# One more step of lag for the head's sums, eight row places instead of four, and an expert number read earlier, in a fused tower of transformer, retention block and mixture of experts

## What is computed

```python
h = tok_ref(x, ...)                                  # 2 layers, band attention, D=192, then LN and a head to 128
h = h + attn_ref(_layernorm(h), ...)                 # retention block, below
h = h + ffn_ref(_layernorm(h), ...)                  # 8 experts, top 1, below

# attn_ref, on x of 128 columns
xn = layernorm(x, ln1_g, ln1_b)
s = a * s + (1 - a) * xn_t                           # scan over time, then ss @ W_out.T + b_out
y_loc = conv(xn, conv_w, 5 taps, per column)
x = x + ss @ W_out.T + b_out + y_loc + conv_b
h = gelu(layernorm(x, ln2_g, ln2_b) @ W1.T + b1)     # 256 wide
x = x + h @ W2.T + b2

# ffn_ref
scores = softmax(xf @ Wg + bg); top_s, top_i = top_k(scores, 1)
out = relu(xf @ W1[e] + b1[e]) @ W2[e] + b2[e]       # e = top_i of the token, 512 wide
return out * top_s
```

## Time and profile before

| what | value |
|---|---|
| time, median of 3 runs (lowest to highest) | 946.12 us (945.46 to 947.41) |
| the profiled execution: its own time / its span | 946.6 us / 944.8 us |
| busy share of the span: PE, PEld, DVE, ACT, POOL | 86%, 66%, 62%, 62%, 59% |
| final stream, from the first sums to the last scatter | 759.6 to 870.3 us |
| tile loop, from the first load's issue to the end | 873.2 to 944.8 us |
| DMA `xt<-xs`: count, issue to landing (min / median / max) | 23, 2.0 / 2.0 / 2.9 us |
| DMA `out<-ot`: count, issue to landing (median) | 23, 2.3 us |

### The profile page before, as it was taken

How to read it: one execution, slowest core, us unless ns; L and a number is a source line. 1 busy time by engine, 2 the same in 40 slices (tenths; PEclk the granted TensorE clock), 3 DMA queues, 4 the chain that set the end, 5 groups by cost and what they waited for, 6 DMA issues and landing times.

```text
span 944.8 us, 23661 instructions
## 1 busy us (share of the span) xinstructions
PE 815.0 (86%) x8467; PEld 619.5 (66%) x8467; DVE 589.8 (62%) x1891; ACT 585.4 (62%) x1622; POOL 553.4 (59%) x819
## 2 busy tenths in 40 slices
PE   5969998999999899898999899999988938983776
PEld 2757767567777565677775567777665727772675
DVE  3868846448987364488873626888534346897343
ACT  3859985248799842378997435799964124662453
POOL 4638876443588664556886625378855355676233
PEclk9989997999999999999999999999989958996899
DMA  2310000602000006120000141100004150001221
GB/s 66 102 43 4 3 16 8 190 6 74 4 3 3 21 23 190 28 85 8 4 3 21 51 141 49 32 4 3 3 3 132 58 202 1 1 29 62 66 74 38
DMA packets 38597, 43.85 MB, mean 46 GB/s; under 512 B 7163, under 2 KB 33882, under 8 KB 38346
## 3 DMA queue, kind: packets, MB, share of 16 engines
q1 hardware_dynamic: 18348, 19.40, 6.8%
q10 hardware_dynamic: 17860, 18.19, 6.1%
q0 software_dynamic: 2272, 4.74, 1.6%
HBM read 20.70 MB, written 21.59 MB: 45 GB/s over the span
## 4 chain that ended last, share of the span: by engine, by line
PE 59%; DVE 13%; ACT 9%; issue 5%; SPq 4%; DMA 4%; POOL 4%; ACTq 1%; POOLq 0%; DVEq 0%
PE bank L1338 7%; PE bank L1475 6%; PE bank L1499 5%; PE bank L1426 4%; PE bank L1544 4%; PE bank L1545 4%; PE bank L1478 3%; PE bank L1364 3%; ACT p L732 3%; PE bank L1375 3%; PE bank L1429 3%; DMA xt<-xs 2%; SPq L453 2%; DVE p L993 2%; PE bank L1390 1%
## 5 line engine op out<-in xcount | busy, mean ns | idle before, releaser
L568 POOL TENSOR_TENSOR p<-p 128x384 f16<-128x384 f32 (+1 forms) x320 | 270.8, 859 | 114.1 <-ACT p L732 105.6
L986 DVE TENSOR_REDUCE nmx<-bank 128x1 f32<-128x384 f32 (+1 forms) x384 | 191.2, 513 | 40.2 <-PE bank L1429 36.1
L731 ACT ACTIVATE p<-bank 128x384 f32<-128x384 f32 (+1 forms) x384 | 174.1, 453 | 46.2 <-PE bank L1478 32.5
L732 ACT ACTIVATE p<-bank 128x384 f16<-128x384 f32 (+1 forms) x384 | 174.1, 453 | 0.0
L1475 PE MATMUL bank<-stack 103*128 103x128 bf16 x1056 | 145.4, 222 | 7.4 <-DMA stack<-mtr 6.0
L1478 PE MATMUL bank<-bandb,idb 128*128 128x128 bf16 x672 | 135.5, 222 | 0.0
L1426 PE MATMUL bank<-stack 100*128 100x384 bf16 (+1 forms) x384 | 120.7, 314 | 1.6 <-DVE nmx L986 1.3
L1499 PE MATMUL bank<-vst,p 128*128 128x49 bf16 x2112 | 115.6, 185 | 1.7 <-POOL p L568 1.7
L1475 PEld LDWEIGHTS bank<-stack 103*128 103x128 bf16 x1056 | 88.4, 99 | 32.0 <-issue 15.6
L1429 PE MATMUL bank<-bandb,idb 128*128 128x128 bf16 x672 | 101.2, 220 | 0.0
L1499 PEld LDWEIGHTS bank<-vst,p 128*128 128x128 f16 x2112 | 91.8, 97 | 11.5 <-POOL p L568 2.1
(11 more groups left out here) (252 smaller groups left out, 1809.7 us busy)
## 6 DMA issues: line engine op xcount, KB each, us to landing
xs<-zrow ACTq DMA_DIRECT2D x8, 2193.0 KB, 11.9
xt<-xs SPq DMA_DIRECT2D x23, 129.0 KB, 2.0
w2s<-in_w SPq DMA_DIRECT2D x4, 576.0 KB
mwbs<-in_mwb SPq DMA_DIRECT2D x1, 2064.0 KB, 8.9
mw2s<-in_mw SPq DMA_DIRECT2D x1, 2048.0 KB, 13.2
lnrow<-in_lnr SPq DMA_DIRECT2D x4, 480.0 KB
stack<-mtr SPq DMA_DIRECT2D x96, 3.0 KB
w1b<-in_w SPq DMA_DIRECT2D x4, 291.0 KB
```

The costliest lines, as they stand in the source:

```text
L568: nc.gpsimd.tensor_tensor(p2[:, u % RING, 0:w], p32[:, u % RING, 0:w], p1[:, u % RING, 0:w], ALU.subtract).then_inc(p2_pool, 1)
L731: nc.scalar.activation(p32[:, s % RING, 0:w], ps[2 + s % 3][:, 0:w], ACT.Exp).then_inc(p32_ready, 1)
L732: nc.scalar.activation(p1[:, s % RING, 0:w], ps[2 + s % 3][:, 0:w], ACT.Exp).then_inc(p1_ready, 1)
L986: nc.vector.tensor_reduce(nmx[:, vn % 3, h:h + 1], nat_bank(v)[:, 0:w], AX.X, ALU.max, negate=True).then_inc(max_done, 1)
```

## The change

Three things, and nothing in the computed values:

1. `DEPTH` goes from 12 to 13, and each lag from that of the head's sums on grows by one on all engines (2 to 3, 3 to 4, and so on up to 12 to 13). The lags of `resid`'s sums (0) and of `z0`, its transposes, `xa`, `xb`, the head's product and `h0` (1) stay. The stream has 29 steps.
2. `XBUF` goes from 4 to 8.
3. In the tile loop VectorE reads the expert number of tile `i + 1` behind `dest` of tile `i`, ahead of its wait for the second product.

```diff
-XBUF, WBUF, OBUF = 4, 3, 4
+XBUF, WBUF, OBUF = 8, 3, 4
...
-DEPTH = 12
+DEPTH = 13
...
@@ VectorE, final stream
-                    i = t - 2
+                    i = t - 3
                     if 0 <= i < NN:
                         dve.wait_ge(kept, i + 1)
                         s_link = ch.mark(nc.vector.bn_stats(sums[:, 1, :], h0[:, i, :]))
...
-                i = t - 4
+                i = t - 5
                 if 0 <= i < NN:
                     b, n = divmod(i, NB)
                     dve.wait_ge(a1_done, i + 1)
...
@@ TensorE, final stream
-                i = t - 5
+                i = t - 6
                 if 0 <= i < NN:
                     b, n = divmod(i, NB)
                     pe.wait_ge(a1_done, min(i + 2, (b + 1) * NB))
...
-                    if t - 8 >= 0:
-                        pe.wait_ge(a2_done, t - 7)
+                    if t - 9 >= 0:
+                        pe.wait_ge(a2_done, t - 8)
...
@@ VectorE, tile loop
+            def expert(i):
+                return dve.value_load(toi[0:1, 0, i:i + 1], min_val=0, max_val=E - 1)
+
+            e = expert(0)
             for i in range(NT + 2):
                 if i < NT:
-                    e = dve.value_load(toi[0:1, 0, i:i + 1], min_val=0, max_val=E - 1)
                     if i >= WBUF:
                         dve.wait_ge(e_relu, i - WBUF + 1)
...
+                if i + 1 < NT:
+                    e = expert(i + 1)
                 if i >= 2:
```

More of the change, by code:

```diff
@@ L614, in _ @@
                     nc.gpsimd.tensor_tensor(x1[:, i, :], x1[:, i, :], bo2b[:, 0, :], ALU.add).then_inc(xb_ready, 1)
-                i = t - 7
+                i = t - 8
                 if 0 <= i < NN:
@@ L803, in _ @@
             for t in range(NN + DEPTH):
-                i = t - 8
+                i = t - 9
                 if 0 <= i < NN:
@@ L816, in _ @@
                                          scale=lfb[0:DHI, 0:1]).then_inc(a0_done, 1)
-                i = t - 3
+                i = t - 4
                 if 0 <= i < NN:
@@ L831, in _ @@
                                          scale=l12[:, 2:3]).then_inc(a2_done, 1)
-                i = t - 11
+                i = t - 12
                 if 0 <= i < NN:
@@ L1115, in _ @@
                 w, p = t % 2, (t - 1) % 2
-                i = t - 6
+                i = t - 7
                 if 0 <= i < NN:
@@ L1120, in _ @@
                     nc.vector.tensor_tensor(x1[:, i, :], ps[4][:, 0:DM], x1[:, i, :], ALU.add).then_inc(y_added, 1)
-                i = t - 10
+                i = t - 11
                 if 0 <= i < NN:
@@ L1581, in _ @@
                     pe.wait_ge(z0_ready, i + 1)
-                    if t - 8 >= 0:
-                        pe.wait_ge(a2_done, t - 7)
+                    if t - 9 >= 0:
+                        pe.wait_ge(a2_done, t - 8)
                     nc.tensor.transpose(ps[0][0:DLO, 0:P], z0[:, i % 2, 0:DLO], idf[:, :])
                     nc.tensor.transpose(ps[0][0:DHI, P:2 * P], z0[:, i % 2, DLO:D], idf[:, :]).then_inc(t0_mm, 1)
-                i = t - 3
+                i = t - 4
                 if 0 <= i < NN:
                     pe.wait_ge(z1_ready, i + 1)
-                    if t - 12 >= 0:
-                        pe.wait_ge(a3_done, t - 11)
+                    if t - 13 >= 0:
+                        pe.wait_ge(a3_done, t - 12)
                     nc.tensor.transpose(ps[1][:, 0:P], z1[:, i % 2, :], idf[:, :]).then_inc(t1_mm, 1)
-                i = t - 12
+                i = t - 13
                 if 0 <= i < NN:
@@ L1599, in _ @@
                         ins.then_inc(lg_mm, 1)
-                i = t - 9
+                i = t - 10
                 if 0 <= i < NN:
@@ L1620, in _ @@
                     nc.tensor.transpose(ps[0][:, 0:P], z2[:, i % 2, :], idf[:, :]).then_inc(t2_mm, 1)
-                i = t - 11
+                i = t - 12
                 if 0 <= i < NN:
                     pe.wait_ge(z3_ready, i + 1)
-                    pe.wait_ge(a1_done, min(t - 2, NN))
+                    pe.wait_ge(a1_done, min(t - 3, NN))
                     nc.tensor.transpose(ps[1][:, 0:P], trow[:, i, 0:DM], idf[:, :]).then_inc(t3_mm, 1)
```

## The result

| | before | after |
|---|---|---|
| time, median (lowest to highest) | 946.76 us, 4 runs (945.46 to 948.02) | 923.98 us, 4 runs (921.13 to 925.23) |
| the profiled execution: own time / span | 946.6 / 944.8 us | 924.96 / 923.2 us |
| ratio, 95% interval | | 0.9755 (0.9726 to 0.9784) |

A forecast was written before the change was run, and what follows sets the result against it. Bound by a ring of VectorE, TensorE and ScalarE in the stream's opening and by late row loads in the tile loop; 4.3 + 13.1 = 17.4 us off the median 946.12 gives 928.7 us, range 924.0 to 936.0.

The forecast's parts named there:

- the ring of two engines: Stream's opening: closed loop of VectorE's `z0`, TensorE's products and ScalarE's copies back to VectorE's sums, 4.43 us a step.
- Opening: Stream's steps 1 to 8: lagging the head's sums makes tapless steps 2.57 us, 23.65 instead of 27.67, gaining 4.02 us.
- the bound of 7.6: Stream up to the tile loop: upper bound of its gain, 7.6 us, if the clock rises before the taps.
- I let it keep that place: End of the stream's steps: `choose` still starts 0.50 us ahead of its step's head product, 4.0 us earlier than before.
- Eight places: Tile loop: loads run eight tiles ahead, tiles take 2.00 us instead of 2.72, tile 20 comes 12.4 us earlier.
- because it is the distance measured within a pair: Tile loop: reason for pricing a tile at 2.00 us, as TensorE starts tile 11 2.00 us behind tile 10.
- The lower bound of 1.96: Tile loop: TensorE's own work, 7.22 us busy over 3.68 tiles in 10 us, 1.96 us a tile.
- End: Behind tile 18's scatter: GpSimd's drained queue bounds the end, 3.38 + 3 x 1.58 = 8.12 instead of 8.78, gaining 0.66 us.
- Longer tiles: Rival, tile loop: some chain holds a tile at 2.35 us, 5.6 us less gain, 934.3 us; chance 0.13.
- Stream gives nothing: Rival, stream: something else sets the opening's step or the clock rises later, the added step eats the gain, 933.0; chance 0.12.
- Early clock: Rival, opening: the denser opening raises TensorE's clock before the taps, 3.3 us more gain, 925.4 us; chance 0.09.
- The output's four places: Rival, tile loop: `ot` waits for the scatter four tiles back, up to 3.37 us a tile, 950.6 us; chance 0.03.

## Why the prediction was right in its mechanism, and which steps failed

The mechanism was right and the sizes were not: the time came out 4.7 us under the forecast and below the range. The step that failed most is the price of a tile, 2.00 us where 1.896 was measured, 1.7 us over 16 tiles. Behind it come `choose` and the slots behind it (0.7 us), the first four tiles (0.95 us, the clock) and the opening (0.4 us); 0.86 us is no effect of the change.

*What bounds.* Right in both stages: the ring of two engines in the opening, the row places in the loop. The kernels with one part each show both.

*Opening.* Forecast 4.02, measured 4.45 in the first pair of traces. The priced steps were nearly exact: 2.54 for 2.57, 5.10 for 5.10, 4.88 for 4.90, 3.16 for 3.37. The 0.2 of the last and 0.05 in each of three full steps (4.01 for 4.06), which I had called unchanged, make the difference. That 4.88 met 4.90 is luck: the clock rose late in both of these traces, and in most others it rose a step earlier (4.06 before, 3.16 with the lag). There the lag is worth 6.3 us instead of 5.43, still inside the bound of 7.6. The wait for `h0` is 3.2 us, a little over the 3 named.

*The rest of the stream.* Here the step "I let it keep that place" failed. In all kernels with the lag `choose` starts 0.91 us ahead of the last head product, not 0.50, and from there to the first scatter it takes 6.82 us instead of 7.38, 0.57 less where 0.3 was counted. These rows of after, PE and DVE, are the place:

```profile
818.84 0.29 PE L1603 MATMUL bank<-wgs,xm 128*128 128x8 f32 x2
...
819.16 0.19 DVE L1088 TENSOR_TENSOR gt<-bank,bgs 128x32 f32<-128x32 f32 x1 [0.28 <-PE bank L1603]
...
820.07 0.49 PE L1620 MATMUL bank<-wca,xa 96*128 96x128 f32 x2 [0.40 <-ACT xb L815]
```

`choose` waits for the router's product, which stands ahead of the head product and waits for none of its copies; tied to it, it was mis-sized by 0.4. Of the 0.57 behind it, `z0` is 0.27, as counted; the rest is one instruction of `choose` (L1096), which took 0.49 us the first time in all three traces of kernels without the lag and 0.18 in those with it, for a reason that is not shown. From the first to the last scatter the stretch shifted whole, as said, within 0.1 us (37.09 and 37.17); from there to tile 0's transpose it took 6.17 us instead of 6.03.

*Clock.* Right that it does not rise before the taps: in none of the kernels with the lag and without added products did it. TensorE's share in the opening rose from 1.88 to 2.22 us of 4.00 and the clock stayed 0.50. With products added inside the steps it was 3.64 of 4.00 and the clock stayed 1.00, which was worth 4.1 us. The Trainium skill ("TensorE: Matmul & The Clock Gate", section "Part 1: The HAM clock gate") says that activity releases the throttle and that the idle state is the throttled one. The runs agree in the direction; here pauses of at most 0.89 us were enough for the clock to fall. What the forecast lacked was the clock's part behind the opening. In the loop it rose some 6 us behind tile 0's transpose instead of 7.6, and tiles 0 to 4 took 8.43 us where 9.4 were counted, 0.95 more gain. That the rise came sooner is seen, not explained, and the gain of 1.82 us in that stretch is partly chance: in the kernels with five or eight places and no products ahead of the tiles those four took 8.43 to 9.32 us, in those with four places 9.59 to 10.91.

*Eight places.* The mechanism is right, and this is the term that was most mis-sized: 2.00 us a tile, measured 1.896, 1.7 us in 16 tiles. The step that failed is "because it is the distance measured within a pair". The first tile of a pair starts behind a wait, and so holds a restart: from its transpose to its first product 0.17 us instead of 0.11, and 0.93 instead of 0.89 for its second product. The second tile of the pair had neither. Part of the 1.7 us needs the third edit too: with the read in its old place 16 tiles took 31.14 us, 0.86 under the forecast's 32.0, and moving it gave the other 0.81. The lower bound of 1.96 was wrong as well: it took TensorE's busy time from a stretch with pauses. That time holds the restarts, and it counts the product ahead of a pause to its end, 1.06 us, where in a run without pauses the next instruction starts 0.89 us behind it. So what passed for TensorE's work was too long. The starts were there to be read in the trace of before, in the second tile of a pair (timeline of PE: transpose, first product, second product):

```profile
898.90 0.27 PE L1637 MATMUL bank<-idf,xt 128*128 128x128 f32 x1
...
899.01 1.06 PE L1645 MATMUL bank<-xtt,wt 128*128 128x128 f32 x8
...
899.90 1.06 PE L1654 MATMUL bank<-mw2s,eht 128*128 x8
```

0.11 us of transpose, 0.89 for eight matmuls, and 0.89 for the other eight, taken as equal since a wait follows them, make 1.89.

*Expert number.* Counted nothing, with the slack named as its worth if tiles became shorter. That is what happened: nothing on four places (0.9999), 0.8 us of the traces on eight (1.2 with the one turn of 2.32).

*End.* 0.45 against 0.66: the last drain took 4.56 us, not 3.38, while the scatters behind it followed at 1.28 to 1.32 instead of 1.58. Two errors that nearly cancel, by luck.

*What lay outside.* 0.86 us of the traces' difference lies ahead of the stream. It is no effect of the change.

*Rivals.* Longer tiles: no. Stream gives nothing: no, 0.54% alone. Early clock: no, only after products were added. The output's four places: VectorE's wait ahead of `ot` is in no list; with DMA engines at 0.40 of the stretch, no contention was seen.

## What to carry to other kernels

Price an engine that is to become the bound from start to start inside a stretch where it runs without a wait, not by its busy time and not by a stretch that begins with a wait. A ring buffer's law is the round trip over the places that are left when those in use are taken off: here 5.2/(n - 2), which put the step between four and five places and made eight no better than five. It holds as long as the round trip itself stays as it was; at three places it grew by the slower clock. And where TensorE waits in short steps, ask whether the clock is part of the price: products that nobody reads, put into the waits themselves, gave 4.1 us in the opening here, and put ahead of them alone 0.75. The whole kernel gained more by the medians, 6.1 and 2.8 us, but 1.3 us of each is a shorter drain, of which no run shows that the products cause it.

## What the runs showed of the hardware

Unexpected was that too few places cost the clock too: 6.77 us a tile instead of 5.2 at three. Unexpected also that, in the kernel with products ahead of the stream alone, the clock fell from 1.00 to 0.50 though no pause of TensorE was longer than 0.89 us; that the same stream has its clock rise in one step or the next, worth 0.8 to 1.9 us in a trace; and that GpSimd's drain behind seven or eight scatters comes in lengths of 3.3 and of 4.5 to 5.3 us.
